# A mixture of experts woven into additive attention: routing weights applied to the up projection's input

## The reference, cut to what matters

```
# additive attention
k = x @ Wx ; q = x @ Wt
h = tanh(q[:, :, None, :] + k[:, None, :, :] + bt)
e = exp(einsum('bijq,qo->bij', h, Wa) + ba[0])
a = e / (sum(e) + EPS) ; v = a @ x ; residual += v
# mixture of 8 experts, 2 of them weighted per token, all computed densely
topk_w = softmax(top_k(x @ router_w.T, 2)) ; dense_w[token, expert] = topk_w or 0
g = x @ w_gate[e] ; u = x @ w_up[e]
y = (silu(g) * u) @ w_down[e]
residual += sum over e of dense_w[:, e] * y[e]
```

## Time and profile before

| what | us |
|---|---|
| median of 3 runs (2186.12 to 2189.18) | 2187.76 |
| the profiled execution's own time | 2195.11 |
| its span, first to last instruction | 2193.2 |
| PE busy, whole span | 1819.4 (83%) |
| DVE busy | 1739.9 (79%) |
| ACT busy | 1300.7 (59%) |
| POOL busy | 301.5 (14%) |

### The profile page before, as it was taken

How to read it: one execution, slowest core, us unless ns; L and a number is a source line. 1 busy time by engine, 2 the same in 40 slices (tenths; PEclk the granted TensorE clock), 3 DMA queues, 4 the chain that set the end, 5 groups by cost and what they waited for, 6 DMA issues and landing times. The chain is left out here.

```text
span 2193.2 us, 31484 instructions
## 1 busy us (share of the span) xinstructions
PE 1819.4 (83%) x11804; PEld 941.7 (43%) x11804; DVE 1739.9 (79%) x4783; ACT 1300.7 (59%) x1355; POOL 301.5 (14%) x360
## 2 busy tenths in 40 slices
PE   6998999898666679999999999999999998654930
PEld 3565655676422124444344444344444464332620
DVE  3667557686777889999999999999999899794632
ACT  1222222332226999999999999999999822010410
POOL 6000012110234000000000000000000000056046
PEclk9879999897778999999999999999999999877975
DMA  5500000000000200000000000000000000031732
GB/s 161 198 1 19 22 18 1 14 2 1 0 0 28 77 1 1 1 1 1 1 1 1 1 1 1 1 1 1 1 1 1 1 1 1 0 151 65 233 95 77
DMA packets 45801, 64.97 MB, mean 30 GB/s; under 512 B 7744, under 2 KB 35921, under 8 KB 44881
## 3 DMA queue, kind: packets, MB, share of 16 engines
q1 hardware_dynamic: 39472, 48.25, 6.7%
q0 software_dynamic: 6176, 14.71, 2.3%
HBM read 37.77 MB, written 23.07 MB: 28 GB/s over the span
## 5 line engine op out<-in xcount | busy, mean ns | idle before, releaser
L2250 ACT ACTIVATE KM<-KM 128x2048 f32<-128x2048 f32 x299 | 583.8, 2066 | 8.0 <-DVE KM L2067 8.0
L2067 DVE TENSOR_SCALAR KM<-big 128x512 f32<-128x512 f32 x1196 | 488.9, 480 | 16.8 <-PE bank L2400 10.7
L2400 PE MATMUL bank<-KM,w_a_wa 128*32 128x512 f32 x2736 | 366.7, 611 | 69.0 <-ACT KM L2250 50.6
L191 POOL TENSOR_TENSOR nrstd<-nrstd,minus_half 128x4 f32<-128x4 f32 (+1 forms) x80 | 78.5, 1005 | 1673.6 <-DVE nrstd L168 1673.5
L2250 ACT ACTIVATE aa_args<-aa_args 128x2048 f32<-128x2048 f32 x149 | 299.5, 2068 | 1.5 <-DVE aa_args L2067 1.5
L2067 DVE TENSOR_SCALAR aa_args<-big 128x512 f32<-128x512 f32 x596 | 244.4, 479 | 1.3 <-PE bank L2400 0.8
L2400 PE MATMUL bank<-aa_args,w_a_wa 128*32 128x512 f32 x1360 | 182.4, 612 | 29.4 <-ACT aa_args L2250 20.9
L2354 PEld LDWEIGHTS bank<-rf_wd,ST 128*128 128x128 f32 x992 | 120.4, 191 | 98.2 <-issue 85.6
L2400 PEld LDWEIGHTS bank<-KM,w_a_wa 128*32 128x32 f32 x2736 | 55.2, 108 | 206.3 <-ACT KM L2250 107.8
L2371 PE MATMUL bank_pair<-XT,rf_wgu 128*128 128x256 f32 x512 | 142.9, 403 | 1.0 <-DVE ST L2139 1.0
L2354 PE MATMUL bank<-rf_wd,ST 128*128 128x128 f32 x992 | 142.8, 287 | 0.4 <-DVE h L2154 0.3
(11 more groups left out here) (440 smaller groups left out, 2861.5 us busy)
## 6 DMA issues: line engine op xcount, KB each, us to landing
queues<-zeros SPq DMA_DIRECT2D x1, 8192.0 KB, 24.3
KM<-queues SPq DMA_DIRECT2D x32, 256.0 KB, 3.7
results<-KM SPq DMA_DIRECT2D x32, 256.0 KB, 3.8
w<-in_w SPq DMA_DIRECT2D x1, 4096.0 KB, 12.6
mf_tv<-in_task_W SPq DMA_DIRECT2D x1, 2048.0 KB, 10.7
la_v<-in_task_W SPq DMA_DIRECT2D x1, 2048.0 KB, 8.6
big<-XN SPq DMA_DIRECT2D x8, 256.0 KB, 2.7
rf_wgu<-in_wgu SPq DMA_DIRECT2D x1, 2048.0 KB, 8.2
```

Of the source, the lines that this page charges most:

```text
L191: self.nc.gpsimd.tensor_tensor(self.m.nrstd[s][:, 0:self.tiles], self.m.nrstd[s][:, 0:self.tiles], self.m.minus_half[:, 0:self.tiles], ALU ...
L2067: last = nc.vector.tensor_scalar(ARG(n, step)[:, cc, :], KU[:, i * T:(i + 1) * T], q, None, ALU.add)
L2250: last = nc.scalar.activation(ARG(n, step), ARG(n, step), ACT.Tanh)
L2400: last = nc.tensor.matmul(m.bank[g][32 * cc:32 * cc + 32, :], w["a_wa"][:, 30 - 2 * k:62 - 2 * k], ARG(n, step)[:, cc, :], start=k == 0, s ...
```

## The change

For the first 14 tiles (`weighted(j)`) the weight of a token is put on the input of the up projection. SP writes WT to a scratch tensor `spread` in memory (128 x 16 floats) and reads it back to every partition (2048 floats each, the view WB on `m.big`). GpSimd multiplies, for each unit, the turned tokens by the weights of two experts, 128x512 into XW(v), one of two buffers (`m.t512b`); in WB the tokens lie 16 floats (64 bytes) apart. PE's ups read XW(v). The products of all eight experts' downs are summed in one PSUM bank, and DVE adds that bank to the residual once per tile (`ADDED`, 128x256) in place of the 16 additions. The begins are 24, 32, 40, 48, and the lags UP (5, 6), MUL 8, LIFTED 12, DOWN (11, 12). The last two tiles keep the old form; the 15th begins at 25, 29, 33, 37. `BIASED` has three steps (9, 16, 25) in place of four.

```diff
-    BIASED = (8, 15, 17, 24)
+    BIASED = (9, 16, 25)
...
-    BEGIN, BEGIN_DRAINED, BEGIN_LAST = (17, 25, 33, 41), (17, 25, 33, 37), (9, 13, 17, 21)
+    BEGIN, BEGIN_DRAINED, BEGIN_LAST = (24, 32, 40, 48), (25, 29, 33, 37), (9, 13, 17, 21)
+    weighted = lambda j: j < LAST - 1
...
-    GATED, UP, TANH, MUL, LIFTED, DOWN, SUM = (0, 1), (2, 3), 3, 7, 8, (6, 7), (14, 15)
-    SUM_DRAINED = (12, 13)
-    sum_of = lambda j: SUM if j < LAST - 1 else SUM_DRAINED
+    GATED, TANH, SUM = (0, 1), 3, (12, 13)
+    UP = lambda j: (5, 6) if weighted(j) else (2, 3)
+    MUL = lambda j: 8 if weighted(j) else 7
+    LIFTED = lambda j: 12 if weighted(j) else 8
+    DOWN = lambda j: (11, 12) if weighted(j) else (6, 7)
+    ADDED = lambda j: begin(j, EP - 1) + (18 if j < LAST - 2 else 15)
...
+    WB = m.big[:, NT * (D + 1) + 2 * PAIRS * T:NT * (D + 1) + 2 * PAIRS * T + E * TOK]
+    XW = lambda v: m.t512b[v % 2][:, :].rearrange("p (x s t) -> p x s t", x=2, s=2)
+    spread = nc.dram_tensor("rf_spread", (P, 2 * E), F32).ap()
+    wt_out, wb_in, xw = sig("wt_out", 16), sig("wb_in", 16), sig("xw", EP)
+    SUMMED = lambda j: m.h[:, tile_of(j):tile_of(j) + NC_ + 1:NC_, :]
...
+            for j in range(LAST - 1):
+                sp.wait_ge(w_sb.sem, w_sb.at(j, 1))
+                if j:
+                    sp.wait_ge(wb_in.sem, wb_in.at(j - 1, 16))
+                sp.dma_start(spread, WT[:, :, :].rearrange("p s e -> p (s e)")).then_inc(wt_out.sem, 16)
+                sp.wait_ge(wt_out.sem, wt_out.at(j, 16))
+                if j:
+                    sp.wait_ge(xw.sem, xw.at(j - 1, EP))
+                sp.dma_start(WB, spread.rearrange("(o t) n -> o (t n)", o=1).broadcast_to([P, E * TOK])).then_inc(wb_in.sem, 16)
...
                 norm2.gpsimd(pool, n)
+                for v in range(EP if weighted(n) else 0):
+                    if v == 0:
+                        pool.wait_ge(wb_in.sem, wb_in.at(n, 16))
+                        pool.wait_ge(x_sb.sem, x_sb.at(n, 1))
+                    if n or v >= 2:
+                        pool.wait_ge(up_ps.sem, up_ps.at(n, v - 1))
+                    nc.gpsimd.tensor_tensor(XW(v), XMT[n % 2][:, 0:TOK].rearrange("p (o s t) -> p o s t", o=1, s=2).broadcast_to([P, 2, 2, P]),
+                                            WB.rearrange("p (t s e) -> p e s t", s=2, e=E)[:, 2 * v:2 * v + 2, :, :], ALU.mult).then_inc(xw.sem, 1)
...
+                if weighted(j) and step == ADDED(j):
+                    dve.wait_ge(dn.sem, dn.at(j, EP))
+                    nc.vector.tensor_tensor(SUMMED(j), SUMMED(j), m.bank[3][:, 0:2 * D].rearrange("p (s d) -> p s d", s=2), ALU.add).then_inc(h_sb.sem, E)
+                for x in range(0 if weighted(j) else 2):
+                    for v in begun(j, step, SUM[x]):
...
+                                if weighted(j):
+                                    last = nc.tensor.matmul(m.bank[3][:, s * D:(s + 1) * D], AC(j, v)[:, x, o:o + P], wd[:, e, a, :],
+                                                            start=e == s == a == 0, stop=e == E - 1 and a == HB - 1, skip_group_check=True)
...
+                        if x == 0 and weighted(j):
+                            pe.wait_ge(xw.sem, xw.at(j, v + 1))
                         for a in range(HB):
-                            last = nc.tensor.matmul(LIFT[:, x, a * TOK:(a + 1) * TOK], wgu[:, e, 1, a, :], XMT[parity][:, 0:TOK], start=True, stop=True)
+                            lifted = XW(v)[:, x, :, :].rearrange("p s t -> p (s t)") if weighted(j) else XMT[parity][:, 0:TOK]
+                            last = nc.tensor.matmul(LIFT[:, x, a * TOK:(a + 1) * TOK], wgu[:, e, 1, a, :], lifted, start=True, stop=True)
```

More of the change, by code:

```diff
@@ L2002, in begun @@
         return [v for v in range(EP) if begin(j, v) + lag == t]
-    assert begin(0, EP - 1) + SUM[1] < CS + 27 and begin(0, EP - 1) + LIFTED < CS + START + 1 and SUM[0] > DOWN[1] + 5
+    WB = m.big[:, NT * (D + 1) + 2 * PAIRS * T:NT * (D + 1) + 2 * PAIRS * T + E * TOK]
[3 more added lines that the diff above has]
+    SUMMED = lambda j: m.h[:, tile_of(j):tile_of(j) + NC_ + 1:NC_, :]
     LATE_EXP, LATE_TURN, LATE_W, ATTEND, ATTENDED = 2, 3, 9, 5, 12
@@ L2132, in route @@
                     dve.wait_ge(wstep.sem, wstep.at(j, 4))
+                    if j and weighted(j - 1):
+                        dve.wait_ge(wt_out.sem, wt_out.at(j - 1, 16))
                     nc.vector.tensor_tensor(WT[:, :, :], top.oh[:, 0:2, :], top.oh[:, 2:4, :], ALU.add).then_inc(w_sb.sem, 1)
@@ L2136, in units @@
             def units(j, step):
-                for v in begun(j, step, MUL):
+                for v in begun(j, step, MUL(j)):
                     dve.wait_ge(th_sb.sem, th_sb.at(j, v + 1))
                     nc.vector.scalar_tensor_tensor(TH, TH, 1.0, GATE[:, :, :], ALU.add, ALU.mult).then_inc(a1_sb.sem, 1)
-                for v in begun(j, step, LIFTED):
+                for v in begun(j, step, LIFTED(j)):
                     dve.wait_ge(a1_sb.sem, a1_sb.at(j, v + 1))
@@ L2145, in units @@
                     nc.vector.tensor_tensor(AC(j, v), TH, LIFT[:, :, :], ALU.mult).then_inc(ac_sb.sem, 1)
-                for x in range(2):
-                    for v in begun(j, step, sum_of(j)[x]):
+                if weighted(j) and step == ADDED(j):
[3 more added lines that the diff above has]
+                    for v in begun(j, step, SUM[x]):
                         e = 2 * v + x
@@ L2182, in iteration @@
                         route(n - 1, before, step)
+                    if n >= 3:
+                        units(n - 3, 2 * CS + step)
                     if n >= 2:
@@ L2342, in units @@
                 for x in range(2):
-                    for v in begun(j, step, DOWN[x]):
+                    for v in begun(j, step, DOWN(j)[x]):
                         e = 2 * v + x
@@ L2346, in units @@
                             pe.wait_ge(ac_sb.sem, ac_sb.at(j, v + 1))
-                            if v or j:
+                            if weighted(j):
+                                if v == 0 and j:
+                                    pe.wait_ge(h_sb.sem, h_sb.at(j, 0))
+                            elif v or j:
                                 pe.wait_ge(h_sb.sem, h_sb.at(j, e - 2 * held(j, v)))
@@ L2353, in units @@
                                 o = a * TOK + s * P
-                                last = nc.tensor.matmul(OUT(j, v, x)[:, s * D:(s + 1) * D], AC(j, v)[:, x, o:o + P], wd[:, e, a, :],
-                                                        start=a == 0, stop=a == HB - 1)
+                                if weighted(j):
+                                    last = nc.tensor.matmul(m.bank[3][:, s * D:(s + 1) * D], AC(j, v)[:, x, o:o + P], wd[:, e, a, :],
+                                                            start=e == s == a == 0, stop=e == E - 1 and a == HB - 1, skip_group_check=True)
+                                else:
+                                    last = nc.tensor.matmul(OUT(j, v, x)[:, s * D:(s + 1) * D], AC(j, v)[:, x, o:o + P], wd[:, e, a, :],
+                                                            start=a == 0, stop=a == HB - 1)
                         if x:
                             last.then_inc(dn.sem, 1)
-                    for v in begun(j, step, UP[x]):
+                    for v in begun(j, step, UP(j)[x]):
                         e = 2 * v + x
```

## The result

| | before | after |
|---|---|---|
| median of 6 runs | 2188.16 (2186.12 to 2189.48) | 2197.21 (2195.21 to 2204.8) |
| the profiled execution, its span | 2195.11, 2193.2 | 2204.8, 2203.0 |
| POOL busy | 301.5 | 435.1 |
| DVE busy | 1739.9 | 1768.2 |
| ACT busy | 1300.7 | 1292.2 |

What follows compares the result with a forecast made beforehand. ACT was taken to bound the kernel before, DVE the changed one; -10.4 - 0.9 + 14.5 + 2.5 = +5.7 us gave 2200.8 for the profiled execution and, 7.35 lower, a median of 2193.5, range 2178 to 2214.

Steps and rivals of the forecast that it cites:

- the multiplications' term: Iterations 2 to 15: DVE's 66.0 against ACT's 64.7, 17.5 us less 3 of DVE's lead, so +14.5 us.
- ACT's saving: One biased step fewer saves 0.65 us in each of 16 iterations, 10.4; one gate tanh leaves iteration 1, 0.9.
- DVE's own work: DVE per iteration without GpSimd: 63.4 + 1.58 for an argument step - 4.16 for additions + 0.34 = 61.2 us.
- The loss per multiplication: DVE standing beside GpSimd on the shared port: 1.2 us for each multiplication, four per iteration, 4.8 us.
- one in four falls on PSUM work: Of each iteration's four multiplications, only the fourth comes near a DVE product with PSUM input, where the loss may be nothing.
- The strided operand: Rival, 20%: XW's 64-byte-apart read lengthens multiplications; 1.6 us lost each gives 2217; decides from 1.3 us lost.
- DVE's load as the period: Attention iterations: DVE's 61.2 + 4.8 = 66.0 us, above ACT's 64.7, sets the period, 1.25 us more per iteration.
- The sign named beforehand: If DVE does not keep up, ACT idles 1 us or more per iteration, with DVE named as releaser of L2250.
- The iterations' sum: Forecast terms of the 16 iterations: -10.4 and -0.9 on ACT, +14.5 for the multiplications.
- The drain: After the iterations: the 15th tile's second unit slides into the last iteration, between 0 and 5.9 us; 2.5 taken.
- The weights' way: WT to memory, back and through POOL takes 8.5 to 9.5 us in all, hidden before PE needs XW(0); cost nothing.
- DVE keeps up: Rival, 33%: a multiplication costs DVE under 0.88 us on average, ACT stays the bound; -8.8 us, 2179.0.

Runs made afterwards that it cites:

- e1: The changed kernel without GpSimd's 56 multiplications, the ups reading the unweighted input; median 2186.91, ratio 1.0004 to the kernel before.
- e2: The changed kernel with GpSimd reading 512 adjacent floats of the weights instead of ones 64 bytes apart; median 2189.1, ratio 1.0007 to the kernel before.
- e6: The changed kernel with a fourth biased step (9, 16, 18, 25); median 2206.84, ratio 1.0078 to the kernel before.
- e9: The changed kernel with PE's attention product two steps later (step 7 in place of 5); median 2191.07, ratio 1.0019 to the kernel before.
- e10: The changed kernel with four biased steps and PE's attention product two steps later; median 2198.54, ratio 1.0057 to the kernel before.
- e3: The changed kernel with each GpSimd multiplication started where DVE's gate product reads PSUM; median 2186.82, ratio 1.0001 to the kernel before.
- e5: The kernel before with the change's begins and a second WT buffer, old weights and sums, four biased steps; median 2198.2, ratio 1.005 to the kernel before.
- e11: e3 with two biased steps (9, 25) and the last weighted tile's sum at lag 18 for 15; median 2171.64, ratio 0.9932 to the kernel before.
- e8: e3 with two biased steps, the 14th tile also in the old form, and earlier begins for 14th and 15th; median 2180.89, ratio 0.9959 to the kernel before.
- e4: The kernel before with three biased steps (8, 16, 24) in place of four, nothing else; median 2183.71, ratio 0.9983 to the kernel before.
- e12: e3 with POOL asking one argument step earlier, amid the arguments ahead of the product; median 2185.45, ratio 0.9994 to the kernel before.

## Why the prediction came out as it did

The median was forecast at 2193.5, and it is 2197.21: the sign and the range were right, the sum was too small by 4, and the mechanism named for the period was not the one. That the sum came so near is in part luck: the multiplications' term was 2.4 too large, the drain's 5 to 7 too small.

- **ACT's saving, right within 1 us.** -10.4 in 16 iterations and -0.9 for the gate tanh moved out make -11.3. e1's iterations are 10.4 shorter at ACT's last attention tanh, and 12.0 at DVE's last argument, since DVE ends 1.6 further ahead there. Its period is 64.78 for a forecast of 64.71.
- **DVE's own work, right.** 61.2 was forecast, e1's window shows 60.98. In the changed kernel 65.71 less 0.44 of waiting less 4.06 of loss is 61.2 too.
- **The loss per multiplication, right in kind, off in size.** 4.8 per iteration was forecast, 4.06 it is. The forecast took 1.2 for each; it is 1.29 for three and 0.17 for the fourth. The reason given for "one in four falls on PSUM work" was wrong: not the last but the first does, and not by where it starts but because its request stands until the product with PSUM input comes.
- **The strided operand, a rival that was half true.** The read 64 bytes apart costs 0.3 us (e2), about a quarter more and not the half of its upper bound (2.0 for 1.32). The mean loss of 1.0 stayed under its point of 1.3.
- **DVE's load as the period: the step that failed.** "DVE's 66.0 against ACT's 64.7" came out near the number (65.71) for another reason. e6 took 1.58 us from DVE and the period rose by 0.65, which is ACT's. With the measured loss DVE's load is 61.2 + 4.06 = 65.3; the 0.4 up to 65.7 is its own waiting. The sign named beforehand, idle time of ACT with DVE as releaser of its tanh, did not come either: ACT stands at the gate's tanh (L2272), released by PE. What ends last is a chain through three engines, DVE and PE each with room of its own. Here it is in the trace of after, PE's timeline and ACT's:

```profile
1164.70 2.15 PE L2341 MATMUL bank<-big,t512c 128*128 128x129 f32 x16 [0.86 <-DVE t512c L2097]
...
1173.62 1.13 PE L2413 MATMUL bank_pair<-XT,rf_wgu 128*128 128x256 f32 x4
```

```profile
1174.79 1.02 ACT L2272 ACTIVATE ST<-bank_pair 128x1024 f32<-128x1024 f32 x1 [0.89 <-PE bank_pair L2413]
```

and PE's wait of after from 900 to 1700, beside ACT's 10.7, 12 times, 0.9 at most, as in e6:

```profile
PE bank L2341 <- DVE t512c L2097: 11.1, 13, 0.9
```

  Two of the three stalls of DVE beside GpSimd (1145.92, 1150.88) lie ahead of the copy of the turned scores (L2097, 1163.97), so that it is late for PE, which walks in order and stands 0.86 us. From there to its gate product, nine us later, PE has no gap, so that this is as much late for ACT, which stands 0.89. 64.8 + 0.9 = 65.7. Moving PE's step (e9, e10) took out 0.6 of it. That the stalls beside GpSimd feed this chain is shown by e1 and e3, where the wait of ACT is absent and the period is ACT's, and by e2, where shorter stalls leave 0.2 of it.
- **The iterations' sum.** +14.5 was forecast for the multiplications, +12.1 measured. With the 12.0 gained, the iterations come out at +0.1 for a forecast of +3.2.
- **The drain, the term that was mis-sized.** 2.5 was taken out of bounds of 0 to 5.9; it is +9.2 from the last argument, +7.5 from ACT's last attention tanh. I priced half of the 15th tile's second unit and left out its first, which begins at 25 for 17 and slides past the end of the attention in part too. PE's work between ACT's last attention tanh and the first copy shows it, in before, e5 and after (window, length, busy us and instructions of PE, PEld, DVE, ACT, POOL):

```profile
1739.50:1789.47 49.97, 46.82 (x290) 36.67 (x290) 39.73 (x102) 11.01 (x16) 0.93 (x2) 1.00 0.01 1
1741.23:1796.62 55.39, 51.48 (x318) 40.29 (x316) 43.14 (x108) 12.03 (x16) 0.87 (x2) 1.00 0.00 1
1741.53:1799.03 57.50, 53.26 (x329) 40.88 (x327) 46.39 (x127) 11.93 (x16) 2.74 (x3) 1.00 0.00 1
```

  PE is busy for all but 3 to 4 us of each. Of the downs (L2354 in before and e5), here with PE and PEld alone, there are 112 before and 128 in e5, one unit more; of the ups 48 and 56:

```profile
1739.50:1789.47 49.97, 14.88 (x112) 13.99 (x112) 1.00 0.01 1
1741.23:1796.62 55.39, 17.23 (x128) 16.16 (x128) 1.00 0.00 1
```

  A unit costs 5.9 there, and e5 shows 5.4 of the 7.5 for the begins alone. The rest, 2.1, is for the most part PE's distance behind ACT. The last scores of the attention, in e5 and in after:

```profile
1741.91 1.07 PE L2400 MATMUL bank<-KM,w_a_wa 128*32 128x512 f32 x8
...
1744.00 1.06 PE L2442 MATMUL bank<-KM,w_a_wa 128*32 128x512 f32 x8
```

  They end 1.8 us and 3.5 us behind the end of ACT's last attention tanh (1741.23 and 1741.53). That the longer lags of the last weighted tile put PE back is likely and was not tried; e11 excludes the late sum. e8 gave 7.0 back with earlier begins and the old form together.
- **The weights' way, right.** 7.5 us were expected, 6.0 measured, and PE's ups never stood for it. DVE's old wait (23.9 us) is gone as forecast.
- **"DVE keeps up" (33%)** has its mechanism confirmed: POOL can wait for its turn and run under PSUM work. The kernel as changed places three of four wrongly; e3 places them all rightly and has this rival's period, 64.79. Even so it is level with before, as the drain takes 9.2 and not 2.5.

With right sizes the sum is -12.0 + 12.1 + 9.2 = +9.3, or, cut at ACT's last attention tanh, -10.4 + 12.1 + 7.5 = +9.2. The stage's difference is 9.30.

## What to carry to other kernels

Place GpSimd's elementwise work by what DVE does at that moment: an instruction that reads PSUM was not lengthened by it, among `tensor_scalar` from and to SBUF each multiplication cost DVE 1.3 of its 1.6 us; and send only one per such place, for the second one behind it met arguments. Two engines with nearly equal loads can be bound by a chain between them, so shift work between them (e6) before believing that the fuller one is the bound. Work begun later in this software pipeline was paid in its drain, 5.4 us for about one unit of 5.9; judge each part of a bundle by itself, since here one biased step fewer made the kernel before 0.17% faster by itself (e4), and the bundle around it made it slower.

## What the runs showed of the hardware beyond that

- A request of GpSimd for a long SBUF operation did not break into a gapless run of DVE's argument instructions. It waited up to 3 us and the arguments kept their pace, in after at the first multiplication of each tile (1141.70) and in e12 at two of each tile (1130.44). Yet the multiplications of 1151.15 and 1169.86 did take their turn among arguments, and so in every tile. What tells the two apart was not tried.
- Where it takes its turn, the DVE instruction that meets it stands for 1.29 us of the multiplication's 1.63: 1.77 for 0.48. With the shorter multiplications of e2 (1.32 to 1.42) it is 1.51.
- A `tensor_tensor` of 128x512 on GpSimd that stood alone took 1.32 us in the earlier trace rows and 1.30 to 1.43 in e2, where no operand is spread, and 1.54 to 1.70 in e3 and after with one of them read 64 bytes apart.
- A DVE instruction of 128x2 with two inputs in SBUF, which met a multiplication in e12, took 1.52 us for 0.16.
- 8 KB out of SBUF into memory took 1.4 us, and the same 8 KB read back to all 128 partitions (1024 KB) 4.6.
